# Attention results brought by transfers to the rows of the projection's input and divided there, in place of two transposes

## The reference

```
zn = (z - mu) / sqrt(var + EPS) * ln_scale + ln_bias
q, k, v = heads(zn @ w_qkv)                  # 16 heads of 16 columns
att = softmax(q k^T / 4)
out = concat(att v) @ w_proj + b_proj
x = x + layernorm(z + out)
# then: x + layernorm(ffn(layernorm(x))), shared expert on all rows, one of 8 experts on 512 rows
```

## Time and profile before

| | |
|---|---|
| median of 3 runs | 1050.6 us (1050.59 to 1052.78) |
| the profiled execution | 1052.78 us |
| its span | 1051.0 us |
| mean granted clock of PE | 0.969 |
| PE, DVE, ACT, POOL busy | 968.4, 838.5, 606.2, 281.3 us |

### The profile page before, as it was taken

One profiled execution on the slowest core, in us unless ns is written; L12 is line 12 of the kernel. 1 busy time (PEld: TensorE's weight loads), 2 busy tenths in 40 slices (PEclk: granted clock), 3 DMA queues, 4 the chain that ended last, 5 costly groups with the idle time before them and its releaser, 6 DMA issues.

```text
span 1051.0 us, 16569 instructions
## 1 busy us (share of the span) xinstructions
PE 968.4 (92%) x6372; PEld 388.1 (37%) x6372; DVE 838.5 (80%) x1634; ACT 606.2 (58%) x700; POOL 281.3 (27%) x418
## 2 busy tenths in 40 slices
PE   4289999999999999999999999999999999966984
PEld 3123333333334334333343343333332333235773
DVE  4287888898887988999879889889899798445765
ACT  3025667677874775767857766667666666731110
POOL 4060001101622231207804412028142020633022
PEclk9697999999999999999999999999999999997998
DMA  5905101320160103200621031003410000231001
GB/s 139 134 1 69 54 2 41 53 70 2 41 93 30 60 22 46 69 9 1 109 94 41 1 45 52 27 1 71 91 60 24 1 2 1 78 133 52 1 1 60
DMA packets 45783, 49.42 MB, mean 47 GB/s; under 512 B 8409, under 2 KB 38889, under 8 KB 45321
## 3 DMA queue, kind: packets, MB, share of 16 engines
q1 hardware_dynamic: 44360, 46.53, 19.7%
q10 hardware_dynamic: 960, 0.79, 0.7%
q0 software_dynamic: 384, 1.05, 0.3%
HBM read 13.94 MB, written 8.91 MB: 22 GB/s over the span
## 4 chain that ended last, share of the span: by engine, by line
PE 83%; DVE 9%; DMA 2%; ACT 2%; issue 2%; POOL 1%; SPq 0%; ACTq 0%; DVEq 0%; POOLq 0%
PE obank L909 23%; PE sc L895 20%; PE ring L877 16%; PE ring L792 10%; PE ring L814 5%; DVE mx L1123 4%; PE sc L984 3%; PE ring L784 3%; PE ring L935 2%; DVE st L1059 2%; ACT prob L720 1%; DMA kp<-parts 1%; PE ring L929 1%; DMA qp<-mp 1%; DMA x_sb<-x 0%
## 5 line engine op out<-in xcount | busy, mean ns | idle before, releaser
L1123 DVE TENSOR_REDUCE mx<-ring 128x1 f32<-128x512 f32 x1024 | 635.1, 681 | 88.0 <-PE ring L877 86.3
L720 ACT ACTIVATE prob<-sc 128x1024 f32<-128x1024 f32 x512 | 495.9, 1021 | 205.4 <-PE sc L895 204.3
L877 PE MATMUL ring<-kp,qp 48*128 48x512 bf16 x1024 | 256.7, 390 | 31.7 <-issue 20.5
L895 PE MATMUL sc<-qp,kp 48*128 48x512 bf16 (+1 forms) x2048 | 274.2, 380 | 2.2 <-DMA qp<-mp 1.4
L909 PE MATMUL obank<-prob,vaug 128*32 128x512 f32 x2048 | 274.4, 608 | 0.7 <-ACT prob L720 0.7
L877 PEld LDWEIGHTS ring<-kp,qp 48*128 48x128 bf16 x1024 | 74.8, 93 | 275.4 <-DVE mx L1123 169.5
L895 PEld LDWEIGHTS sc<-qp,kp 48*128 48x128 bf16 (+1 forms) x2048 | 99.4, 95 | 105.4 <-ACT prob L720 20.0
L531 POOL TENSOR_TENSOR resid<-qkf,parts 128x1024 f32<-128x1024 f32 x8 | 17.1, 2132 | 207.7 <-ACT parts L668 207.7
L482 POOL TENSOR_TENSOR sum_m<-st 128x8 f32<-128x8 f32 x15 | 3.1, 209 | 257.3 <-DVE st L1059 257.3
L909 PEld LDWEIGHTS obank<-prob,vaug 128*32 128x32 f32 x2048 | 40.3, 108 | 65.1 <-issue 61.7
L537 POOL TENSOR_SCALAR parts<-resid 128x1024 bf16<-128x1024 f32 x14 | 14.7, 1050 | 181.2 <-DVE resid L1113 180.4
(11 more groups left out here) (190 smaller groups left out, 827.3 us busy)
## 6 DMA issues: line engine op xcount, KB each, us to landing
kp<-parts SPq DMA_DIRECT2D x96, 128.0 KB, 5.0
qp<-parts SPq DMA_DIRECT2D x180, 64.0 KB, 2.6
x_sb<-x SPq DMA_DIRECT2D x7, 1024.0 KB, 5.7
out<-hid SPq DMA_DIRECT2D x4, 1024.0 KB, 4.5
x_scratch<-x SPq DMA_DIRECT2D x3, 1024.0 KB, 4.7
qp<-mp SPq DMA_DIRECT2D x128, 2.0 KB
kp<-ew SPq DMA_DIRECT2D x1, 2048.0 KB, 8.2
x_sb<-x SPq DMA_DIRECT2D x2, 512.0 KB, 4.6
```

The lines of the kernel that those rows point to most:

```text
L720: nc.scalar.activation(prob[:, e % 2, 2 * a:2 * a + 2, :].rearrange("p g n -> p (g n)"), sbuf2[a][:, :], ACT.Exp, scale=0.25).then_inc(s_f ...
L877: nc.tensor.matmul(dst[:, :], qp[rows, qh, h, qt * P:(qt + 1) * P], kp[rows, h, kh * HALF:(kh + 1) * HALF], start=True, stop=True).then_in ...
L895: ins = nc.tensor.matmul(dst[:, j * HALF:(j + 1) * HALF], kp[rows, h, kt * P:(kt + 1) * P], qp[rows, qh, h, :], start=plane == 0, stop=pla ...
L1123: nc.vector.tensor_reduce(mx[:, u % 2, n:n + 1], src[:, :], AX.X, ALU.max).then_inc(rv_free, 1)
```

## The change

`oT` is no longer transposed. SP's `result_rows` sends, for each unit, the 16 rows of each of its four heads from `oT` straight to the rows of `yA` that the projection reads (columns of the result along the partitions), and one transfer that spreads each sum row over the 16 rows of its head in `sums`. Two groups of heads fill 128 partitions, so after every second unit of a half DVE's `divide` makes the reciprocal of `sums[:, qh]`, 128x512, in place and multiplies the 128x512 of `yA`. Items "ot" and "a" fall away, with ACT's copies of "a"; `p` reads `yA`. Divisions stand in slots 41 and 47 and, for the batch before, 14 and 16; the last two stand behind the loop, with two of the last unit's row transfers on ACT's queue. The "z" items of batches 1 and 2 move from slots 10 to 13 to 14 to 17. `pick`, a constant of POOL, is made later and in the memory of `qkf`, and gathered rows use `yA`.

```diff
-Z_AT = (14, 10)
+Z_AT = (14, 14)
 V_AT = (22, 25, 50, 51)
 P_AT = (20, 21, 23, 24)
-
-HALVES = (0, 2, 1, 3)
 H_AT = (44, 45, 47, 48)
 
 
 F_AT = ((4, 5), (0, 1))
+
+
+D_AT = (41, 47, 14, 16)
+
+ROWS = 16 * (1 + GH)
...
-        if 1 <= w < B and 16 <= tau < 20:
-            fill.append(("a", w - 1, tau - 16))
...
-        if e >= 0 and e % 8 == 2 and 0 <= e // 8 - 1 < B * HU:
-            row.append(("ot", e // 8 - 1))
...
-    at[SLOTS] = ([("a", last, i) for i in HALVES] + [("p", last, i) for i in range(4)]
+    at[SLOTS] = ([("p", last, i) for i in range(4)]
...
-        anat = sb("anat", [P, NT, D])
+        yA = sb("yA", [P, KD, N])
+        sums = sb("sums", [P, NH, HALF])
...
+            def result_rows(u):
+
+                b, g, qh = u // HU, u % HU // NH, u % NH
+                n = 4 * b + 2 * (g // 2) + qh
+                row, cols = GH * HD * (g % 2), slice(qh * HALF, (qh + 1) * HALF)
+                sp.wait_ge(s_oT, u + 1)
+                if u % HU == 0 and b > 0:
+                    sp.wait_ge(r_full, R_INDEX["p", b - 1, 3] + 1)
+                if g % 2 == 0 and n >= 2:
+                    sp.wait_ge(s_div, n - 1)
+                sp.dma_start(sums[row:row + GH * HD, qh, :],
+                             oT[HD:P:VW, u % 2, :].rearrange("p (o n) -> p o n", o=1).to_broadcast([GH, HD, HALF]))\
+                  .then_inc(s_rows[qh], 16)
+                for i in range(GH if u < B * HU - 1 else GH // 2):
+                    sp.dma_start(yA[row + i * HD:row + (i + 1) * HD, g // 2, cols],
+                                 oT[i * VW:i * VW + HD, u % 2, :]).then_inc(s_rows[qh], 16)
...
+                for u in range(B * HU):
+                    if t == 8 * u + SL // HU + LEAD + (4 if u % HU == 0 else 1):
+                        result_rows(u)
...
+                    if u >= NH:
+                        sc.wait_ge(s_rows[u % NH], ROWS * (u // NH))
...
+            u = B * HU - 1
+            sc.wait_ge(s_oT, u + 1)
+            for i in range(GH // 2, GH):
+                nc.scalar.dma_start(yA[GH * HD + i * HD:GH * HD + (i + 1) * HD, KD - 1, HALF:N],
+                                    oT[i * VW:i * VW + HD, u % 2, :]).then_inc(s_rows[1], 16)
...
-                elif kind == "a":
-                    if key[2] == 0:
-                        pe.wait_ge(rv_free, TAKEN["ot", HU * b + HU - 1][1] + 1)
-                    transpose_in(key, anat, key[2] // NH, key[2] % NH)
                 elif kind == "p":
-                    if key[2] == 0:
-                        pe.wait_ge(ra_free, TAKEN["a", b, 2 if b == B - 1 else 3][1] + 1)
-                    if key[2] == 2 and b == B - 1:
-                        pe.wait_ge(ra_free, TAKEN["a", b, 3][1] + 1)
-                    project(key, yT, key[2], wp, KD)
+                    if key[2] == 0 or key[2] == 2 and b == B - 1:
+                        pe.wait_ge(s_div, 4 * b + (3 if key[2] == 0 and b == B - 1 else 4))
+                    project(key, yA, key[2], wp, KD)
...
-                if e >= 0 and e % 8 == 2 and 0 <= e // 8 - 1 < B * HU:
-                    u = e // 8 - 1
-                    dst = open_r("ot", u)
-                    pe.wait_ge(s_oT, u + 1)
-                    for c in range(QT):
-                        ins = nc.tensor.transpose(dst[:, c * P:(c + 1) * P], oT[:, u % 2, c * P:(c + 1) * P], ident[:, :])
-                    ins.then_inc(r_full, 1)
...
+            def divide(b, kk, qh):
+                last_u = HU * b + (2 * kk + 1) * NH + qh
+                cols = slice(qh * HALF, (qh + 1) * HALF)
+                ve.wait_ge(s_rows[qh], ROWS * (last_u // NH + 1))
+                nc.vector.reciprocal(sums[:, qh, :], sums[:, qh, :]).then_inc(s_recip, 1)
+                ve.wait_ge(s_recip, 4 * b + 2 * kk + qh + 1)
+                nc.vector.tensor_tensor(yA[:, kk, cols], yA[:, kk, cols], sums[:, qh, :], ALU.mult).then_inc(s_div, 1)
...
-                elif kind == "ot":
-                    u = key[1]
-                    b, g, qh = u // HU, u % HU // NH, u % NH
-                    src = take_r(*key)
-                    o = src[:, :].rearrange("p (c n) -> p c n", n=VW)
-                    ve.wait_ge(rv_free, TAKEN[key][1])
-                    if u % HU == 0 and b > 0:
-                        ve.wait_ge(r_full, R_INDEX["a", b - 1, 3] + 1)
-                    nc.vector.reciprocal(rsum[:, :], o[:, :, HD]).then_inc(s_rs, 1)
-                    ve.wait_ge(s_rs, u + 1)
-                    o4 = src[:, :].rearrange("p (q h n) -> p q h n", h=GH, n=VW)
-                    r4 = rsum[:, :].rearrange("p (q h o) -> p q h o", h=GH, o=1).to_broadcast([P, QT, GH, HD])
-                    a4 = anat[:, qh * QT:(qh + 1) * QT, g * GH * HD:(g + 1) * GH * HD]\
-                        .rearrange("p q (h d) -> p q h d", h=GH)
-                    nc.vector.tensor_tensor(a4, o4[:, :, :, 0:HD], r4, ALU.mult).then_inc(rv_free, 1)
...
+                if tau in D_AT:
+                    kk, qh = divmod(D_AT.index(tau), NH)
+                    if 0 <= w - kk and w < B:
+                        divide(w - kk, kk, qh)
...
+            divide(last, 1, 0)
             for i in range(4):
                 h = i // 2
+                if i == 1:
+                    divide(last, 1, 1)
```

More of the change, by code:

```diff
@@ L100 @@
 R_INDEX = {item: i for i, item in enumerate(RING)}
-BY_ACT = ("z", "qk", "v", "a", "x", "u", "te", "tg")
+BY_ACT = ("z", "qk", "v", "x", "u", "te", "tg")
 TAKEN = {}
@@ L177, in build @@
         ident = sb("ident", [P, P])
-        pick = sb("pick", [E, E, P])
         iota = sb("iota", [P, E])
@@ L213, in build @@
         pickb = resid[:, HALF:N].bitcast(bf16).rearrange("p (e n) -> p e n", e=E)
-        xg, xgn = anat[:, 0:MT, :], anat[:, MT:2 * MT, :]
+        xg, xgn = (yA[:, i, :].rearrange("p (t d) -> p t d", d=D) for i in range(2))
+        pick = qkf[0:E, :].rearrange("p (e n) -> p e n", e=E)
         mhid = x_sb[:, 0:MT, :]
@@ L266, in build @@
         s_oT = sem("output_evacuated")
-        s_rs = sem("reciprocal_sums")
+        s_rows = [sem("result_rows_first_half"), sem("result_rows_second_half")]
+        s_recip = sem("reciprocal_sums")
+        s_div = sem("results_divided")
+        s_clear = sem("weight_rows_cleared")
         s_x1 = sem("x1_ready")
@@ L451, in _ @@
                                     base=0, pattern=[[-1, P]], channel_multiplier=1).then_inc(s_made, 1)
-            nc.gpsimd.affine_select(out=pick[:, :, :], in_=pick[:, :, :], compare_op=ALU.not_equal, fill=1.0,
-                                    base=0, pattern=[[-1, E], [0, P]], channel_multiplier=1)\
-                .then_inc(s_made, 1)
             nc.gpsimd.memset(vaug[:, :, :, :], 0.0).then_inc(s_small, 1)
-            pool.wait_ge(s_made, 2)
+            pool.wait_ge(s_made, 1)
             pool.wait_ge(s_small, 1)
@@ L599, in _ @@
             pool.wait_ge(s_third, 2 * KD * B)
-            nc.gpsimd.memset(ohTb, 0.0)
-            nc.gpsimd.memset(resid[:, HALF:N], 0.0).then_inc(s_wide, 1)
+            nc.gpsimd.memset(resid[:, HALF:N], 0.0)
+            step(nc.gpsimd.memset(pick, 0.0))
+            nc.gpsimd.affine_select(out=pick, in_=pick, compare_op=ALU.not_equal, fill=1.0, base=0,
+                                    pattern=[[-1, E], [0, P]], channel_multiplier=1).then_inc(s_wide, 1)
             z_with_bias(B - 1)
+            pool.wait_ge(s_pickb, 1)
+            nc.gpsimd.memset(ohTb, 0.0).then_inc(s_clear, 1)
             for k in ("y", "x"):
@@ L607, in _ @@
             pool.wait_ge(s_x1st, 16 * (B + 1))
-            pool.wait_ge(r_full, R_INDEX["a", B - 1, 3] + 1)
+            pool.wait_ge(r_full, R_INDEX["p", B - 1, 3] + 1)
             pool.wait_ge(s_idx, 7)
@@ L731, in _ @@
             last = B - 1
+            u = B * HU - 1
[3 more added lines that the diff above has]
+                                    oT[i * VW:i * VW + HD, u % 2, :]).then_inc(s_rows[1], 16)
             for key in RING_AT[SLOTS]:
-                if key[0] in ("a", "x"):
+                if key[0] == "x":
                     ring_item(key)
@@ L913, in _ @@
                 for key in RING_AT[t]:
-                    if key[0] not in ("max", "mt", "ot"):
+                    if key[0] not in ("max", "mt"):
                         ring_item(key)
@@ L929, in _ @@
                     nc.tensor.transpose(dst[0:GH * QT, 0:P], nm[:, u % 2, :], ident[:, :]).then_inc(r_full, 1)
-                if e >= 0 and e % 8 == 2 and 0 <= e // 8 - 1 < B * HU:
-                    u = e // 8 - 1
-                    dst = open_r("ot", u)
-                    pe.wait_ge(s_oT, u + 1)
-                    for c in range(QT):
-                        ins = nc.tensor.transpose(dst[:, c * P:(c + 1) * P], oT[:, u % 2, c * P:(c + 1) * P], ident[:, :])
-                    ins.then_inc(r_full, 1)
             last = B - 1
             for key in RING_AT[SLOTS]:
-                if key[0] in ("a", "p", "x") or key[0] == "h" and key[2] < 3:
```

(7 more changed lines are left out.)

6 lines of the change are left out of this document (removed).

## The result

| | before | after |
|---|---|---|
| median | 1050.61 us | 1127.82 us (4 runs, 1127.14 to 1129.43) |
| ratio to before, 95% interval | | 1.0735 [1.0717, 1.0753] |
| span of the profiled execution | 1051.0 | 1125.3 |
| mean granted clock of PE | 0.969 | 0.922 |
| first to last value product (the loop) | 836.7 | 890.9 |

The change costs 77 us, where the forecast was 32 and the range ended at 1102. Of the 74.3 us between the spans, 54.2 lie in the loop, 18.7 in the tail and 1.4 ahead of the first value product (92.4 us against 91.0).

A forecast was written before the change was run, and what follows sets the result against it. DVE was taken to bound plain slots, PE those with extra PE work. Loop +15.7, clock +14 and tail +2.0 made +31.7 us, 1082.3 against the median, said as 1083; range 1064 to 1102.

The forecast's parts named there:

- the main mechanism: Loop: divisions hold DVE about 4.0 us each, PE idles about 3 us, and its clock falls to half level behind most.
- DVE's time, less what goes (loop): Loop: fourteen divisions cost 48.9 us uncovered on DVE, less 33.2 for the removed items: +15.7 us.
- clock (loop): Loop, behind divisions: PE's idleness drops its clock to half level, 1.0 us each, +14 us (0 to 30).
- the divided tail: Behind the loop: the last division waits for transfers, then delays the projection and the last addition: +2.0 us.
- B: Divisions: the reciprocal runs an element a cycle like other 128x512 operations, a division takes 1.3 us: 1027, chance 0.08.
- C: Divisions: the reciprocal takes eight steps an element, 4.3 us, a division 5.0: 1098, chance 0.08.
- A: Loop: the clock holds, with no half-level stretch or one wholly in the stall: 1068, chance 0.17.
- D: SP's queue: five more transfers among the stacking ones make rows of maxima late, scores wait, +22 us: 1105, chance 0.06.
- The transfers: SP's queue: five transfers a unit, with slack behind the evacuation wait; zero cost, up to 5 us.
- What goes: Loop: removed "ot" items save 26.1 us and "a" items 7.1, in all 33.2 us before the tail.

The follow-up runs named there:

- The first run: Changed kernel with the last load of x and the store of batch 2's output ahead of the last result transfers on SP: 1111.68 us.
- the third run: Changed kernel with POOL's bias addition for batches 0 to 2 held back until the batch's last division is done: 1117.95 us, ratio 1.0632.

## Why the prediction was wrong

The direction was right (0.89 for slower) and so was the main mechanism; 1083 missed 1127.8, and the range missed it too. Term by term, measured against the spans:

| term | predicted | measured |
|---|---|---|
| DVE's time, less what goes (loop) | +15.7 | +19.7, with order, POOL and clock taken out |
| clock (loop) | +14 (0 to 30) | 24.1 |
| POOL's addition (loop) | none | 8.9 |
| the divided tail | +2.0 | +3.0 |
| the load of `x` behind SP's wait (tail) | none ("I put zero, with up to 5") | 15.7 |
| ahead of the loop | none | +1.4 (the other kernels: 90.2 to 93.9, before 91.0) |

They add up to 72.8 of the 74.3.

**Right.** The reciprocal, in no row before, was taken as 3.35 us from two small ones; it is 3.343. That the pace is by columns was reasoned; that the middle of two readings (3.1 and 3.5) comes out to 7 ns is luck. The division holds DVE for 4.0. Slots with one last 6.5 to 8.0 us where nothing else comes in (6.5 to 7.7 were said), and plain slots stay at 2.48. The rivals with another reciprocal, B and C, are out. So is A: the clock did not hold, sixteen value products between 150 and 905 us take over 1.25 us, where before it was one, and PE's waits for maxima, as said, became long (before, then after; us in all, times, longest us):
```profile
PE ring L877 <- DVE mx L1123: 8.1, 15, 1.3
```
```profile
PE ring L896 <- DVE mx L1143: 51.1, 28, 7.1
```
D did not happen in its form: the scores' waits for rows of maxima sum to 0.8 us, and the loop has no more than 1.5 us that other terms leave open.

**The step that failed** is "The transfers": "Behind SP's wait for the evacuation stand the stacking of keys and queries and the rows of maxima". That is true in the loop. At its end, other things stand there: the last load of `x`, the store of batch 2's output and the loads of the experts' weights. I listed what is queued behind the wait in the place that I was looking at, and not in the last place where the same wait stands. The first run shows 15.7 us for it, and nothing but the order was changed.

**A term that was absent.** I counted the multiplication at 0.69 us from a row in which POOL was idle. The operation before it read PSUM, through `ring`; the new one has both inputs in SBUF, and POOL adds the bias just then. Worth 8.9 us, shown by the third run, and by a 16-column multiplication that lasts 3.69. The Trainium skill ("SBUF — State Buffer", "Who interferes with whom") says that a DVE instruction with two SBUF inputs contends with a GpSimd instruction that reads SBUF, that the ports they share are an exclusive lock, and that the order of issue decides who blocks. By that rule the trace's 3.71 us had to be looked for, and the trace agrees: POOL began 1.34 us before the multiplication, which ended 0.55 us after it. I had not weighed it.

**A size that was off.** The clock's place was right: half level behind the stalls, and 4.2 to 6.3 us for the slot behind. I took 1.0 us a division, between 0 and 3.1; 24.1/14 = 1.7 is measured. The slot of the earlier trace rows had been 1.57 above plain, and I had taken a third off because part of the low stretch would lie inside the stall. The low clock lies in the stretch in which PE works again: behind batch 0's slot 41 the granted clock is 0.50 from 184.0 to 187.6 us, with PE busy all the while.

**A count that was off.** What goes is some 31 us, not 33.2. The slot behind an "ot" slot still has 2.61 us in thirteen places of the changed kernel, so its 0.13 was not the "ot" item's; the sum had it fifteen times, 2.0 in all. Of the rest of the 4.0 us in the first line, 1.4 is in batch 0, where slots 48 and 49 are still that much longer with the clock kept up; what makes them so was not tried, and 0.6 stays open.

Without the two absent terms the kernel would have been at 1127.8 - 15.7 - 8.9 = 1103.2, just beyond the range's end of 1102. That is an estimate; no run has these two edits alone.

## What to carry to other kernels

Price a moved operation with what else runs at its new place: what POOL does while DVE reads two operands from SBUF, and what an idle PE does to the clock behind it; here 4 us of DVE in one piece cost a slot and the slot after. Where a wait is added to an in-order queue, read on to the end of the program, past the loop, and list what stands behind its last instance. And an operation whose time goes by columns per partition wants its data spread over partitions first: with the sums in 128x16, SP's order mended and the products placed clear of POOL's sums, the change that had cost 7.3% gained 1.1%.

## What the runs showed of the hardware

- A reciprocal in f32 goes by columns: 178 ns for 4, 257 for 16 read from PSUM, 241 for 16 from SBUF, 3343 for 512, so (3343 - 178)/508 = 6.2 ns for each further one (5.3 from 4 to 16). On 64 partitions 512 columns took the same 3.35 us. An f32 addition of two 128x512 takes 692 ns in all.
- A DVE multiplication of two SBUF operands stood until POOL's sum of two tensors was over (0.69 us became 3.71 and 4.22, and 0.175 became 3.69). The reciprocal at 299.87, under the same POOL operation for its last 1.3 us, kept its 3.34; and in the third run POOL's addition began at 313.99, beside four reductions, which read PSUM and kept their 2.48:
```profile
313.75 2.48 DVE L1145 TENSOR_REDUCE mx<-ring 128x1 f32<-128x512 f32 x4
```
- Stalls of about 3 us, one at each of fourteen divisions, cost the changed kernel 24.1 us in the loop by PE's clock, which fell to its half level (1.2 GHz); useless matmuls in the stalls brought that back, net of their own time. In the kernel before, fourteen holds of 3.1 us took the granted clock between 160 and 700 us from 1.00 to 0.97, and the slots behind them were 18.5 us longer.
- A hold's price does not end with it: in the stretch behind slot 14's hold of 7 us (columns as above) the mean granted clock is 0.56, so most of it is at the half level.
```profile
308.10:311.50 3.40, 3.40 (x17) 1.14 (x18) 1.25 (x4) 0.33 (x1) 0.00 (x0) 0.56 1.11 128
```
